# Scores of an edge batch stored by type and head, and a search moved to the batches without a mix tile

## The reference

```python
K, Q, V = projections by node type        # (n, 8 heads, 32)
Ks, Qt, Vs = K[src], Q[tgt], V[src]       # 50000 edges
for t in range(3):                        # edge types
    mask = edge_types == t
    scores = sum((Ks @ Wa[t]) * Qt, -1) * inv_sqrt_dk * relation_pri[t]
    scores = where(mask[:, None], scores, -inf)
    w = softmax(scores, axis=0)           # over all edges, by type and head
    msgs += where(mask[..., None], w[..., None] * (Vs @ Wm[t]), 0)
agg = segment_sum(msgs.reshape(-1, 256), tgt, num_segments=n)
```

## Time and profile before

| | us |
|---|---|
| median of 3 runs (1034.78 to 1035.46) | 1035.15 |
| the profiled execution | 1035.89 |
| its span, first to last instruction | 1034.1 |
| busy in the span: PE / DVE / ACT / POOL | 859.6 / 794.3 / 601.2 / 600.0 |
| granted TensorE clock, mean | 0.922 |

### The profile page before, as it was taken

One profiled execution on the slowest core, in us unless ns is written; L12 is line 12 of the kernel. 1 busy time (PEld: TensorE's weight loads), 2 busy tenths in 40 slices (PEclk: granted clock), 3 DMA queues, 4 the chain that ended last, 5 costly groups with the idle time before them and its releaser, 6 DMA issues.

```text
span 1034.1 us, 18416 instructions
## 1 busy us (share of the span) xinstructions
PE 859.6 (83%) x5153; PEld 633.9 (61%) x5153; DVE 794.3 (77%) x1682; ACT 601.2 (58%) x1540; POOL 600.0 (58%) x745
## 2 busy tenths in 40 slices
PE   4999999993887778877778778777769778999998
PEld 3777777762454455555555555554449666888886
DVE  6755666653788899999999999999878647997441
ACT  2655766662566798788798877896642122322221
POOL 4605777766677677777777776777730337662000
PEclk9999999996678998899898988997889989999999
DMA  9823665666788788888888887888726812320020
GB/s 284 260 85 113 240 220 210 220 218 225 243 247 260 237 262 241 262 257 260 258 258 247 276 255 234 264 261 248 238 70 188 256 57 89 95 72 6 2 97 27
DMA packets 126204, 202.76 MB, mean 196 GB/s; under 512 B 19755, under 2 KB 94846, under 8 KB 126102
## 3 DMA queue, kind: packets, MB, share of 16 engines
q0 software_dynamic: 38992, 129.87, 39.7%
q1 hardware_dynamic: 76630, 61.86, 19.7%
q10 hardware_dynamic: 10480, 9.83, 2.9%
HBM read 160.50 MB, written 40.99 MB: 195 GB/s over the span
## 4 chain that ended last, share of the span: by engine, by line
PE 41%; DVE 20%; POOL 14%; issue 10%; DMA 8%; ACT 4%; SPq 1%; DVEq 0%; ACTq 0%; POOLq 0%
POOL big L1394 9%; PE ps L2404 5%; PE ps L914 5%; DVE big L1818 4%; DMA big<-kv_scratch,src_i 4%; PE ps L1610 4%; PE ps L2391 4%; PE ps L1593 3%; PE ps L955 3%; PE ps L926 2%; PE ps L902 2%; DVE big L1758 2%; DVE ps L1765 2%; PE ps L2355 2%; POOL big L2253 2%
## 5 line engine op out<-in xcount | busy, mean ns | idle before, releaser
L1394 POOL DMA_INDIRECT big<-kv_scratch,src_i x392 | 372.6, 950 | 138.3 <-issue 113.6
L1593 PE MATMUL ps<-edge 64*128 64x256 f32 x784 | 130.2, 456 | 61.6 <-DVE big L1758 35.7
L1610 PE MATMUL ps<-big,edge 128*64 128x256 f32 x784 | 130.7, 463 | 35.0 <-DVE big L1818 34.8
L1593 PEld LDWEIGHTS ps<-edge 64*128 64x128 f32 x784 | 82.2, 216 | 102.7 <-issue 69.1
L1758 DVE TENSOR_TENSOR big<-big,ps 128x1024 f32<-128x1024 f32 x98 | 119.1, 1216 | 16.1 <-DMA big<-kv_scratch,src_i 13.2
L1765 DVE TENSOR_REDUCE ps<-big 128x32 f32<-128x1024 f32 x98 | 120.1, 1225 | 2.5
L1818 DVE TENSOR_TENSOR big<-big,ps 128x1024 f32<-128x1024 f32 x98 | 118.0, 1205 | 0.0
L1471 ACT ACTIVATE edge<-edge 128x64 f32<-128x64 f32 x392 | 103.8, 338 | 1.6
L2317 ACT ACTIVATE big<-ps,fb 128x256 f32<-128x256 f32 (+2 forms) x104 | 39.5, 462 | 103.5 <-PE ps L2391 103.5
L1610 PEld LDWEIGHTS ps<-big,edge 128*64 128x64 f32 x784 | 55.3, 158 | 67.8 <-DVE big L1818 44.9
L2391 PE MATMUL ps<-big 128*128 128x256 f32 (+2 forms) x416 | 90.4, 373 | 2.8 <-ACT big L2304 2.8
(11 more groups left out here) (346 smaller groups left out, 1724.0 us busy)
## 6 DMA issues: line engine op xcount, KB each, us to landing
edge<-q_scratch SPq DMA_DIRECT2D x196, 64.0 KB
big<-kv_scratch,src_i POOLq DMA_INDIRECT x392
edge<-key_scratch SPq DMA_DIRECT2D x98, 64.0 KB
agg_scratch<-big SPq DMA_DIRECT2D x16, 252.0 KB
xn_scratch<-big ACTq DMA_DIRECT2D x5, 640.0 KB, 3.5
mix_scratch<-big SPq DMA_DIRECT2D x25, 128.0 KB, 1.8
mix_x_scratch<-big SPq DMA_DIRECT2D x25, 128.0 KB, 1.8
wmix<-mix_x_scratch ACTq DMA_DIRECT2D x25, 128.0 KB, 2.7
```

Of the source, the lines that this page charges most:

```text
L1394: pool.indirect_dma_start(kv_slots[s][:, k, :], None, kv_d[0:N, :], bass.IndirectOffsetOnAxis(ap=src_i[:, e:e + 1], axis=0)).then_inc(got[ ...
L1593: ins = pe.matmul(qr_ps[g % 2][:, (2 * hg + k) * D:(2 * hg + k + 1) * D], ohT[64 * hg:64 * hg + 64, g % 2, k * P:(k + 1) * P], qwin[64 * h ...
L1610: ins = pe.matmul(sums_of(g)[64 * hg:64 * hg + 64, :], oneh[:, g % OHRING, k, hg * 64:hg * 64 + 64], kv_slots[s][:, 2 * hg + k, D:2 * D], ...
```

## The change

Three edits, all in the edge stage. The scores `s3` are stored as 24 columns j by 9 tiles k, k innermost; `scores_of` gives that view, and `mark`, `maxima`, `subtract`, the exponential and the two constants use it. The sums of `head_sums` in PSUM (`scr`) are stored by head, tiles innermost. What the exponential writes, and all behind it, keeps its order. The search's steps leave the batches with a mix tile: a batch without one, from batch 6 on, has two, one behind `products(2b + 1)` and one at its end. So batches 6 and 7 have steps 0 to 3, the twelve batches 10, 13, 16 and so on to 43 have steps 4 to 27, and 45, 46 and 47 the last five.

```diff
--- before.py
+++ after.py
@@ -1329,6 +1329,9 @@
 
             h_ps_e, y_ps_e = ps[0][:, 0:D], ps[0][:, D:2 * D]
 
+            def scores_of(b):
+                return s3[:, b % 2, :].rearrange("p (j k) -> p j k", k=BT + 1)
+
             def odd_kept(b):
                 return min(2 * b, NG - 4)
 
@@ -1481,7 +1484,8 @@
                     act.wait_ge(sbt, b + 1)
                     at_least(act, zz, b - 1)
                     at_least(act, ws, b - 1)
-                    act.activation(ex[:, b % 2, :], s3[:, b % 2, 0:BT * TH], ACT.Exp).then_inc(exd, 1)
+                    act.activation(ex[:, b % 2, :].rearrange("p (k j) -> p k j", j=TH),
+                                   scores_of(b)[:, :, 0:BT].rearrange("p j k -> p k j"), ACT.Exp).then_inc(exd, 1)
 
                 def keep_rows(g):
                     if not in_range(g):
@@ -1762,29 +1766,26 @@
                     if not in_range(g):
                         return
                     dve.wait_ge(pr, g + 1)
-                    dve.tensor_reduce(scr[:, g // 2 % 2, (g % 2) * EG * H:(g % 2 + 1) * EG * H].rearrange("p (k h) -> p k h", h=H),
+                    dve.tensor_reduce(scr[:, g // 2 % 2, :].rearrange("p (h k) -> p k h", k=BT)[:, (g % 2) * EG:(g % 2 + 1) * EG, :],
                                       kv_slots[g % RING][:, :, 0:D].rearrange("p k (h d) -> p k h d", d=DK), AX, ALU.add
                                       ).then_inc(sc, 1)
 
-                def tiles_by_type(b):
-                    return s3[:, b % 2, 0:BT * TH].rearrange("p (k j) -> p k j", j=TH)
-
                 def mark(b):
                     if not in_range(2 * b):
                         return
                     dve.wait_ge(sc, 2 * b + 2)
                     at_least(dve, exd, b - 1)
-                    dve.tensor_tensor(s3[:, b % 2, 0:BT * TH].rearrange("p (k t h) -> p k t h", t=ETY, h=H),
-                                      scr[:, b % 2, :].rearrange("p (k t h) -> p k t h", t=1, h=H).to_broadcast([P, BT, ETY, H]),
-                                      mask3[:, BT * b:BT * (b + 1), :].rearrange("p k (t h) -> p k t h", h=1)
-                                      .to_broadcast([P, BT, ETY, H]), ALU.add).then_inc(mk, 1)
+                    dve.tensor_tensor(s3[:, b % 2, :].rearrange("p (t h k) -> p t h k", t=ETY, h=H)[:, :, :, 0:BT],
+                                      scr[:, b % 2, :].rearrange("p (t h k) -> p t h k", t=1, h=H).to_broadcast([P, ETY, H, BT]),
+                                      mask3[:, BT * b:BT * (b + 1), :].rearrange("p k (t h) -> p t h k", h=1)
+                                      .to_broadcast([P, ETY, H, BT]), ALU.add).then_inc(mk, 1)
 
                 def maxima(b):
                     if not in_range(2 * b):
                         return
                     dve.wait_ge(mk, b + 1)
                     at_least(dve, mT, b - 1)
-                    dve.tensor_reduce(mx[:, b % 2, 0:TH], s3[:, b % 2, :].rearrange("p (k j) -> p j k", j=TH), AX, ALU.max
+                    dve.tensor_reduce(mx[:, b % 2, 0:TH], scores_of(b), AX, ALU.max
                                       ).then_inc(mxd, 1)
 
                 def maximum(b):
@@ -1798,8 +1799,8 @@
                         return
                     dve.wait_ge(mB, b + 1)
                     at_least(dve, ye, odd_kept(b))
-                    v = tiles_by_type(b)
-                    dve.tensor_tensor(v, v, mB_ps.rearrange("p (k j) -> p k j", k=1).to_broadcast([P, BT, TH]), ALU.subtract
+                    v = scores_of(b)[:, :, 0:BT]
+                    dve.tensor_tensor(v, v, mB_ps.rearrange("p (j k) -> p j k", k=1).to_broadcast([P, TH, BT]), ALU.subtract
                                       ).then_inc(sbt, 1)
 
                 def weights(b):
@@ -1821,8 +1822,8 @@
 
                 dve.wait_ge(s_end, 2)
                 dve.memset(mall[:, :], 0.0)
-                dve.memset(s3[:, 0, BT * TH:(BT + 1) * TH], EMPTY)
-                dve.memset(s3[:, 1, BT * TH:(BT + 1) * TH], EMPTY)
+                dve.memset(scores_of(0)[:, :, BT:BT + 1], EMPTY)
+                dve.memset(scores_of(1)[:, :, BT:BT + 1], EMPTY)
                 c(dve.memset(mx, 0.0))
                 dve.sem_inc(s_ed, 1)
                 dve.tensor_scalar(neg_key, keyb[:, :], -1.0, None, ALU.mult).then_inc(s_nk, 1)
@@ -1918,11 +1919,19 @@
 
                 first_index(c)
                 float_bases(c)
+                steps = list(range(SEARCH_STEPS))
+
+                def next_search():
+                    if b >= SEARCH_AT and steps:
+                        search(c, steps.pop(0), 1)
+
                 for b in range(NB):
                     products(2 * b)
                     head_sums(2 * b)
                     subtract(b - 1)
                     products(2 * b + 1)
+                    if not mix_tiles(b, 1):
+                        next_search()
                     for m in mix_tiles(b, 1):
                         mix_row(m)
                     head_sums(2 * b + 1)
@@ -1937,8 +1946,9 @@
                     for m in mix_tiles(b, 1):
                         mix_var(m)
                         mix_gain(m)
-                    if b >= SEARCH_AT:
-                        search(c, b - SEARCH_AT, 1)
+                    if not mix_tiles(b, 1):
+                        next_search()
+                assert not steps
                 subtract(NB - 1)
 
                 def negate_maximum(chain):
```

## The result

The median is 1028.56 us (nine runs) against 1035.15 for the kernel before (nine runs of the same session): a ratio of 0.9941, with an interval of 0.9912 to 0.9969, or 6.1 us less (the two medians differ by 6.6). The forecast was 11.3 us less. **The sign was right; the gain was a little over half of what was forecast**, and the time lies inside the range near its upper end. It is outside the 1019.5 to 1026 of the forecast's own case. It stands where the costly form was put, 1026 to 1031, and that rival's mechanism did not happen, as the next rows show. The profiled execution took 1032.54 us (span 1030.8) against 1035.89 (span 1034.1).

The account below looks back on a forecast made before the run. GpSimd's gathers were taken as the floor, the slot ring's round as the pace; 10.85 us gained mid-stage, 0.5 at the start, 0.3 lost at the end, with a little more 11.3: 1035.15 - 11.3 = 1023.8 us, range 1018 to 1029.

Parts of the forecast that it names:

- the forecast's own case: Whole kernel: the edits gain about 11.3 us, so the time falls in 1019.5 to 1026; chance 0.62.
- the costly form: Edge stage, VectorE: mark and subtract each 0.22 us longer, gain 7 us, time 1026 to 1031; chance 0.16.
- The forms: VectorE's changed instructions: maxima 0.25 us shorter each, mark and subtract 0.03 longer each, head sums unchanged.
- The bound by the gathers: Edge stage: GpSimd's gathers need 30.05 us per three batches; waits total 20.5, the most the stage can shrink.
- three periods: Edge stage, three batches: gather-slot ring 31.12 us, VectorE 30.35, GpSimd 30.05; the longest sets the pace.
- the round of the ring: Edge stage, gathers through VectorE to slot-freeing matmuls and the next gather: 31.12 us falls to 30.18 per three batches.
- the residual of 0.35: Gathers from 357.22 to 722.77: loss per three batches falls from 1.28 us to 0.35, so 10.85 gained.
- its slower rival: Edge stage, TensorE: closer packing puts lower-clock stretches in more mix batches, up to 2.6 us each; chance 0.05.
- The exponential's cover: ScalarE: strided reading costs 0 to 0.22 us a batch, covered up to about 1 us because VectorE needs it late.
- The start and the early batches: Edge stage up to 357.22: the wait at 273.78 loses 0.5 us, the 3.22 at 357.22 stays; 0.8 gained.
- The signs named: Profile after: maxima near 0.38 us, few short GpSimd waits, VectorE waiting for gathers in most batches, last gather near 740.
- the forecast for the search: Steps moved to batches without mix tile are covered; a GpSimd wait behind such a batch would show it wrong.

Follow-up runs that it names:

- the repeats: The changed kernel run and profiled twice more with no edit: 1025.90 us, 0.9914, and 1025.83 us, 0.9941, against the kernel before.
- the kernel in storage order: Changed kernel with exponential, weights, messages and totals also following the scores' new order: 1025.21 us, 0.9912 of the kernel before; again 1020.58 us, 0.9892.

## Why the prediction was right or wrong

**The forms: right.** 0.255 us saved in each `maxima` (0.25), `mark` and `subtract` 0.001 and 0.004 longer (0.03 taken), the head sums nothing. In the profile VectorE is busy 11.3 us less in all. Of the two prices weighed, the row of 372 ns was the right guide. The Trainium skill ("Vector Engine (DVE) Microarchitecture Reference", section 5.2, "Measured stream behaviour on trn2") wants pairs of words on an 8-byte boundary for the full rate. By the prediction's estimate from its figures `mark` would have come out some 0.13 and `subtract` some 0.05 longer than by the rows; the trace does not agree, with 348 and 351 ns. The step of 64 words in the kernel in storage order (371 ns) says the same.

**The bound by the gathers: right as a bound, wrong as the next in line.** That VectorE's seconds wouldn't come through one for one held: 18.0 us put back cost 4.3, none of it in the middle stretch, and the search's move gained 6.3 of the gathers' stretch with none saved. But the prediction named three periods (ring, VectorE, GpSimd) and took the largest of them, and there was a fourth. Its step "the round of the ring becomes 31.12 - 2 x 0.25 - 0.44 = 30.18" and the residual of 0.35 chosen from it failed: 0.73 was measured, and 0.69 and 0.57 in the repeats. The step assumed that once the ring's round is short nothing stands above GpSimd's 30.05. The chain over TensorE, ScalarE and VectorE's messages holds 30.58 in a round; ScalarE is busy 300.5 of the 355 us from 360 to 715. It was hidden before (taking the loads away moved nothing) and shows after: a quarter fewer gathers leave the later rounds at 30.5 to 30.9, 12.8 us more of VectorE leave the middle stretch as it is, and leaving out half of `mix_h`'s matmuls and a part of `mix_y`'s brings most later rounds to 30.0. That there is such a period, and that TensorE's work is in it, is therefore shown. 11.7 x (0.73 - 0.35) = 4.4 us: this is the term that was missized, more than the whole difference of 2.7 us in the gathers' stretch (11.3 forecast, 8.6 measured), because the early batches gave 2.8 where 0.8 was taken. Over all their profiles the gathers fell from 509.9 to 501.2, by 8.7.

**What makes the fourth period: partly open.** ScalarE's part is on the chain but few of its seconds come through: 64 us fewer bring 2 at most, 26 us more cost 1.2. Then another path of nearly the same length is met, the ring of sixteen gathers with 30.48. The stretches at the granted clock of 0.50 lie in both paths, and freeing ahead of each of the twelve waits of GpSimd falls into one; it takes 1.97 us there against 1.08, and the wait beyond the issue is 0.61, so by this sum it would be gone without the lower clock. That is argued from the rows and not shown, as no run sets the clock. The mean clock from 360 to 715 us was 0.89 in the first and third profile of the changed kernel and 0.91 in the second, 0.92 and 0.93 before; but with less of TensorE's work it was 0.88, and 34 of the freeing matmuls' sets seen from 360 to 715 us took over 1.6 us where the changed kernel has 18 to 20, with one of the shortest rounds. So the clock alone doesn't order the kernels, and slow freeing costs little where the rest of the path is short. The prediction had this as its slower rival, with "closer packing brings such stretches to more mix batches"; it came in small. Nor is the longer exponential the whole cause, since running it twice cost nothing that can be told from the spread. Why everything in storage order then gains some 5 us (496.4 on average in the gathers against 501.2, 3.5 of it in the middle stretch) is not settled: its edits weren't tried one by one.

**The exponential's cover: wrong in the reason, nearly harmless in size.** It took 547 ns, at the upper end of the 0 to 0.22 given. The prediction said it was covered because VectorE asks for it late. The row of `weights` bears that out (0.3 us of idle time in 49). But ScalarE has its own queue, and TensorE waits for the one-hot rows behind it. Who waits for the engine next, not only who waits for this result, was the question to ask. The chain after has it with 0.55 in a round.

**`mix_row`'s wait: not weighed.** Each mix batch of the sum holds the 0.35 that L1904 waits for TensorE, taken as fixed. It goes with TensorE and not with VectorE. After the change L1905 waits 5.9 us in 14 batches from 370 to 715, 0.42 each; less work on VectorE doesn't make it earlier.

**The start and the early batches: too small.** 2.8 us instead of 0.8. The wait at 273.78 fell from 2.33 to 1.83, the 0.5 forecast. The 3.22 at 357.22, which the prediction left, is 0.30 in this profile. It is no fixed wait: a second profile of the kernel before has 1.02 there and 2.23 at 305.65, with the same start (115.7), and the repeats of the changed kernel have 1.30 and 0.30 there. That the start became shorter by the layout is shown by the part tried alone; why by more than the 0.8 is open. **The end: right in sign**, 0.7 later and not 0.3, with a wait of 1.08 at 734.27.

**The signs named.** Maxima at 0.38: yes. Waits of GpSimd few and short: short (1.37 at most), but still one in each round. They stand behind mix batches, as the forecast for the search asked. VectorE waiting for a gather in most batches: no, 12 times in 34 batches, because it waits for TensorE and ScalarE instead; this sign was the first that pointed to the fourth period. Last gather near 740: 743.0, 743.0 and 740.0.

**From the stage to the whole.** The span follows the last gather one for one only on average. The part behind it took 280.1 to 287.8 us in 16 profiles of all kernels, with no order by what was changed (the changed kernel itself: 287.8, 280.2 and 285.4). The first profiled execution of the changed kernel had the 287.8, so its span alone would have put the gain at 3.3 us. The ratios of all runs put it at 6.1 to 8.9 us.

## What to carry to other kernels

Before pricing a saved wait, walk once round the loop on every engine, not only on those that the chain names: an engine busy 85% of the time, with results in its queue that others wait for, has a period of its own, and here it stood some 0.5 us behind the one removed. When a change has two parts, try each alone and compare by stretch: here the parts alone add up to what was forecast for the middle stretch (11.0 against 10.85), and the two together do not reach it. When a layout changes, price its reading by each engine separately: what was free to VectorE made ScalarE's instruction half as long again. And compare stretches with fixed ends (first to last gather) before spans, and more than one profile of each.

## What the runs showed of the hardware

- VectorE read or wrote runs of 8 words out of 9, and a bf16 mask at a step of 6 bytes, at the price of what is in order (347 to 351 ns for 192 in a tensor-tensor). A reduction of 192 single words 8 or 64 apart in threes took 371 to 372 ns, some 0.03 us over an estimate in order (369 ns for 216, less 24 at 1.07 ns). The step of 24 words in nines was dear, 624 against 369 ns for 216.
- ScalarE pays for its steps: 192 elements took 358 to 363 ns in order, 547 reading at a step of 9 words (0.96 ns more an element), and 663 writing at a step of 24 words.
- Nearly the same code (the kernel in storage order differs there by a few small instructions) took 280.1 to 287.8 us behind the last gather, with the granted clock of a 28 us window at 0.65 in one execution and 0.82 in another.
